# A graph-attention layer on one core: TensorE operands swapped in seven of eight blocks, with the start's order changed

## The reference

```python
# x: 4096 x 128 float32, adj: 4096 x 4096 int32, attn: 256 x 1
s_i = emb @ attn[:d]
s_j = emb @ attn[d:]
e = leaky_relu(s_i + s_j.T, negative_slope=0.2)
e = e + where(adj > 0, 0.0, -1e9)
alpha = softmax(e, axis=1)
out = layernorm(x + alpha @ emb, axis=-1)     # eps 1e-5, emb = x
```

## Time and profile before

| | us |
|---|---|
| median of 3 runs | 259.89 (259.09 to 260.67) |
| the profiled execution's own time | 261.14 |
| its span in the trace | 259.4 |
| PE busy | 249.2 (96%) |
| PEld busy | 241.6 (93%) |
| VectorE busy | 234.4 (90%) |
| ScalarE busy | 169.0 (65%) |
| POOL busy | 36.2 (14%) |
| HBM read and written | 69.21 MB and 2.10 MB, 275 GB/s over the span |

### The profile page before, as it was taken

How to read it: one execution, slowest core, us unless ns; L and a number is a source line. 1 busy time by engine, 2 the same in 40 slices (tenths; PEclk the granted TensorE clock), 3 DMA queues, 4 the chain that set the end, 5 groups by cost and what they waited for, 6 DMA issues and landing times.

```text
span 259.4 us, 5385 instructions
## 1 busy us (share of the span) xinstructions
PE 249.2 (96%) x2117; PEld 241.6 (93%) x2117; DVE 234.4 (90%) x383; ACT 169.0 (65%) x250; POOL 36.2 (14%) x74
## 2 busy tenths in 40 slices
PE   7899999999999999999999999999999999999980
PEld 6556999999999999999999999999999999999970
DVE  1858999999999999999999999999999999999252
ACT  0579999976975797559954795559752986154010
POOL 1000000000330033003300330015000330033022
PEclk9999999999999999999999999999999999999997
DMA  6999999999999999999999999999999991001001
GB/s 202 316 347 348 349 348 347 350 349 346 349 349 357 351 349 359 352 350 320 326 359 345 329 272 364 339 337 295 361 315 326 264 252 42 3 0 44 0 0 44
DMA packets 70237, 71.68 MB, mean 276 GB/s; under 512 B 2881, under 2 KB 68674, under 8 KB 70210
## 3 DMA queue, kind: packets, MB, share of 16 engines
q1 hardware_dynamic: 34594, 34.67, 44.3%
q10 hardware_dynamic: 34592, 34.67, 43.6%
q0 software_dynamic: 1024, 1.97, 2.3%
HBM read 69.21 MB, written 2.10 MB: 275 GB/s over the span
## 4 chain that ended last, share of the span: by engine, by line
PE 89%; ACT 3%; DMA 2%; DVE 1%; POOL 1%; SPq 1%; ACTq 1%; issue 0%; DVEq 0%
PE psum L808 86%; DMA x_raw<-in_x_dram 2%; PE psum L786 1%; PE psum L775 1%; POOL out_dram L259 1%; ACT adj_in L357 1%; ACT mask_bytes L386 1%; ACTq L251 1%; ACT q_row L369 1%; SPq L233 0%; ACT x_raw L470 0%; DVE weights L674 0%; ACT xj L375 0%; DVE mask_t L583 0%; ACT adj_in L348 0%
## 5 line engine op out<-in xcount | busy, mean ns | idle before, releaser
L808 PEld LDWEIGHTS psum<-xj,weights 128*128 128x128 f32 x2048 | 229.1, 192 | 1.5 <-issue 0.9
L808 PE MATMUL psum<-xj,weights 128*128 128x129 f32 x2048 | 229.8, 275 | 0.2 <-DVE weights L674 0.2
L674 DVE SCALAR_TENSOR_TENSOR weights<-q_row,r_j,mask_t 128x512 f32<-128x512 f32 x256 | 172.6, 740 | 1.6
L392 ACT ACTIVATE mask_bytes<-adj_in 128x4096 uint8<-128x4096 int32 x27 | 97.5, 3611 | 28.6 <-DMA adj_in<-in_adj_dram 28.6
L570 DVE STREAM_TRANSPOSE mask_t<-mask_bytes 128x1024 uint32<-128x1024 uint32 x27 | 33.4, 1236 | 0.0
L312 POOL TENSOR_SCALAR neg_mean<-total 128x4 f32<-128x4 f32 x7 | 3.2, 460 | 169.4 <-ACT x_raw L398 169.4
L398 ACT ACTIVATE x_raw<-x_raw 128x128 f32<-128x128 f32 x28 | 8.3, 297 | 22.5 <-DVE x_raw L619 22.5
L321 POOL DMA_DIRECT2D out_dram<-x_raw x28 | 14.6, 527 | 20.5 <-ACT x_raw L412 20.4
L386 ACT ACTIVATE mask_bytes<-adj_in 128x2048 uint8<-128x2048 int32 x9 | 17.1, 1909 | 0.0
L405 ACT ACTIVATE unused<-x_raw,neg_mean 128x128 f32<-128x128 f32 x28 | 10.9, 391 | 4.1 <-POOL neg_mean L312 4.1
L412 ACT ACTIVATE x_raw<-x_raw,offset,rstd 128x128 f32<-128x128 f32 x28 | 11.5, 480 | 2.3 <-POOL offset L318 2.3
(11 more groups left out here) (58 smaller groups left out, 59.8 us busy)
## 6 DMA issues: line engine op xcount, KB each, us to landing
adj_in<-in_adj_dram ACTq DMA_DIRECT2D x64, 512.0 KB, 13.4
adj_in<-in_adj_dram SPq DMA_DIRECT2D x64, 512.0 KB, 13.6
out_dram<-x_raw POOLq DMA_DIRECT2D x28, 64.0 KB, 5.4
x_raw<-in_x_dram ACTq DMA_DIRECT2D x4, 128.0 KB, 3.1
x_raw<-in_x_dram SPq DMA_DIRECT2D x4, 128.0 KB, 3.6
x_raw<-in_x_dram ACTq DMA_DIRECT2D x2, 256.0 KB, 5.8
x_raw<-in_x_dram SPq DMA_DIRECT2D x2, 256.0 KB, 7.1
out_dram<-x_raw POOLq DMA_DIRECT2D x4, 32.0 KB, 1.9
```

The lines of the kernel that those rows point to most:

```text
L392: nc.scalar.activation(mask_bytes[:, g % BYTE_SLOTS, :, :, :], adj_in[:, g % ADJ_SLOTS, :, :, :], ACT.Sign).then_inc(bytes_ready, 1)
L674: nc.vector.scalar_tensor_tensor(weights[:, slot_of(n, c), :], q_row[:, n * BANK:(n + 1) * BANK], r_j[:, c:c + 1], mask_t[:, (n * PIECES + ...
L808: return nc.tensor.matmul(banks[(n * K + t) % 8][:, 0:D1], weights[:, slot_of(n, c), t * P:(t + 1) * P], xj[:, c, 0:D1], start=(c == 0), s ...
```

## The change

It does four things.

1. In blocks 0 to 6 the operands on TensorE are swapped: `xj` of the chunk (128 columns) is stationary and the chunk's 512 weights are the moving operand, one product for a chunk (`block_product`) in place of four. The sums of a block come out with features on partitions and rows along the free axis, in one bank. After a block, ScalarE copies them to SBUF (`take_sums`, 128 x 512), and TensorE turns them back by four transposes (`turn_back`), right after chunk 6 of the next block; `residual` reads those, at chunk 19 in place of 13.
2. 128 columns must now hold the denominator too. `xj` drops the last feature: columns 0 to 126 are `(x - x_127) * d_j`, column 127 is `d_j`. A shift of all features of a row is taken out by the LayerNorm, so feature 127 of `y` is left as `x_127`. `scale_xj` therefore becomes Identity with a bias and a scale operand for each partition; the bias `-x_127 * d_j` is made on POOL. The last block keeps four products for a chunk, now of 128 columns, not 129.
3. At the start, the load of `attn` is issued on SP behind the two transfers of the first `x` part, not before them.
4. Of piece 0's first half, ScalarE converts two of four tiles and VectorE the two others. ScalarE's `q_piece(1)` to `(7)` move behind pieces 3, 4, 5 and 6 (before: 1 to 3 at once, the rest behind pieces 2 and 4). The LayerNorm steps of a block move to fixed distances behind its `take_sums`.

```diff
-    D1 = D + 1
-    PITCH = D + 2
+    DEN = D - 1
...
+    BY_DVE_TILES = 2
...
-    RESIDUAL_AT = 13
+    TURN_BACK_AT = 6
+    RESIDUAL_AT = 19
+    TAKE_SUMS_AT = [4, 9, 13, 18, 22, 27, 31]
+    SUM_ROWS_IN = 3
+    NORMALISE_IN = 4
...
+    SUM_BANK = [3, 2]
+    BACK_BANK = [1, 0]
...
         def _(sp):
 
+            load_x(sp, LOW_HALF, 0)
             sp.dma_start(attn_row_in[:], attn[:, :].rearrange("d o -> o d")).then_inc(attn_loaded, 16)
-            for part in range(X_PARTS):
+            for part in range(1, X_PARTS):
                 load_x(sp, LOW_HALF, part)
...
+            pool.wait_ge(products_ready, STRIPES)
+            nc.gpsimd.tensor_scalar(neg_last[:], x_raw[:, :, DEN], -1.0, 0.0, ALU.mult, ALU.add).then_inc(neg_last_ready, 1)
+            pool.wait_ge(neg_last_ready, 1)
+            pool.wait_ge(factors_ready, 1)
+            nc.gpsimd.tensor_tensor(last_x[:], neg_last[:], d_j[:], ALU.mult).then_inc(last_x_ready, 1)
+            nc.gpsimd.tensor_copy(xj[:, :, DEN], d_j[:]).then_inc(xj_last_ready, 1)
...
-            nc.scalar.activation(xj[:, :, D], below_max[:], ACT.Exp, scale=SLOPE)
...
-                    nc.scalar.activation(xj[:, c, 0:D], x_raw[:, c, :], ACT.Copy, scale=d_j[:, c:c + 1]).then_inc(xj_scaled, 1)
+                    nc.scalar.activation(xj[:, c, 0:DEN], x_raw[:, c, 0:DEN], ACT.Identity, bias=last_x[:, c:c + 1],
+                                         scale=d_j[:, c:c + 1]).then_inc(xj_scaled, 1)
...
+            def take_sums(n):
+
+                act.wait_ge(weights_used, (n + 1) * CHUNKS)
+                if n > 0:
+                    act.wait_ge(turned_back, n)
+                nc.scalar.copy(sums[:], banks[SUM_BANK[n % 2]][:, :]).then_inc(sums_ready, 1)
...
+            act.wait_ge(adj_loaded[0], 16 * Q)
+            nc.scalar.activation(mask_bytes[:, 0, BY_DVE_TILES:K, :, 0:P], adj_in[:, 0, BY_DVE_TILES:K, :, 0:P],
+                                 ACT.Sign).then_inc(quarter_by_act_ready, 1)
             q_piece(0)
-            act.wait_ge(factors_ready, 1)
+            act.wait_ge(last_x_ready, 1)
             scale_xj(0, 1)
-            q_piece(1)
-            q_piece(2)
-            q_piece(3)
...
-                if g == PIECES - 2:
-                    q_piece(4)
-                    q_piece(5)
-                elif g == PIECES:
-                    q_piece(6)
-                    q_piece(7)
-                if g % PIECES == PIECES - 1 and g > PIECES:
-                    sum_rows(g // PIECES - 1)
-                    sum_squares(g // PIECES - 1)
-                if g % PIECES == 0 and g > PIECES:
-                    normalise(g // PIECES - 2)
+                if g == PIECES - 1:
+                    q_piece(1)
+                elif g >= PIECES and 2 * (g - PIECES) + 2 < RB:
+                    q_piece(2 * (g - PIECES) + 2)
+                    q_piece(2 * (g - PIECES) + 3)
+                if g - SUM_ROWS_IN in TAKE_SUMS_AT:
+                    sum_rows(TAKE_SUMS_AT.index(g - SUM_ROWS_IN))
+                    sum_squares(TAKE_SUMS_AT.index(g - SUM_ROWS_IN))
+                if g - NORMALISE_IN in TAKE_SUMS_AT:
+                    normalise(TAKE_SUMS_AT.index(g - NORMALISE_IN))
+                if g in TAKE_SUMS_AT:
+                    take_sums(TAKE_SUMS_AT.index(g))
...
+            def turn_back(n):
+
+                pe.wait_ge(sums_ready, n + 1)
...
+                for t in range(K):
+                    last = nc.tensor.transpose(banks[BACK_BANK[n % 2]][:, t * P:(t + 1) * P], sums[:, t * P:(t + 1) * P], ident[:])
+                last.then_inc(turned_back, 1)
+
+            def block_product(n, c):
+                nc.tensor.matmul(banks[SUM_BANK[n % 2]][:, :], xj[:, c, :], weights[:, slot_of(n, c), :],
+                                 start=(c == 0), stop=(c == CHUNKS - 1)).then_inc(weights_used, 1)
+
+            def product(c, t):
+                return nc.tensor.matmul(banks[((BLOCKS - 1) * K + t) % 8][:, 0:D], weights[:, slot_of(BLOCKS - 1, c), t * P:(t + 1) * P],
+                                        xj[:, c, :], start=(c == 0), stop=(c == CHUNKS - 1))
...
+                    if n > 0 and c == TURN_BACK_AT:
+                        turn_back(n - 1)
```

More of the change, by code:

```diff
@@ L598, in group_of, with sums_of @@
                 return FINAL_GROUPS if n == BLOCKS - 1 else [slice(0, K)]
+            def sums_of(n, t):
+                if n == BLOCKS - 1:
+                    return banks[(n * K + t) % 8][:, 0:P]
+                return banks[BACK_BANK[n % 2]][:, t * P:(t + 1) * P]
             def denominators(n, g):
                 v = group_of(n)[g]
[L602 to L608 removed]
+                if n < BLOCKS - 1:
+                    dve.wait_ge(turned_back, n + 1)
+                    den = banks[BACK_BANK[n % 2]].rearrange("p (t d) -> p t d", d=P)[:, :, DEN]
+                else:
+                    if v.stop < K:
+                        dve.wait_ge(tile_summed, v.stop)
+                    else:
+                        dve.wait_ge(weights_used, (n + 1) * CHUNKS)
+                    bank = (n * K + v.start) % 8
+                    den = psum[:, bank:bank + v.stop - v.start, DEN]
+                nc.vector.tensor_scalar(rden[:, v], den, LEAST, None, ALU.max).then_inc(den_ready, 1)
             def invert(n, g):
@@ L805, in _ @@
                 s_i_piece(rb)
-            def product(n, c, t):
-                return nc.tensor.matmul(banks[(n * K + t) % 8][:, 0:D1], weights[:, slot_of(n, c), t * P:(t + 1) * P],
-                                        xj[:, c, 0:D1], start=(c == 0), stop=(c == CHUNKS - 1))
+            def turn_back(n):
+                pe.wait_ge(sums_ready, n + 1)
+                if n < 2:
+                    pe.wait_ge(q_ready, S_I_BANK.index(BACK_BANK[n]) + 1)
+                else:
+                    pe.wait_ge(y_ready, (n - 1) * K)
+                for t in range(K):
[7 more added lines that the diff above has]
+                                        xj[:, c, :], start=(c == 0), stop=(c == CHUNKS - 1))
             for n in range(BLOCKS):
@@ L816, in _ @@
                         pe.wait_ge(xj_scaled, c + 1)
+                        if c == 0:
+                            pe.wait_ge(xj_last_ready, 1)
                     pe.wait_ge(weights_ready, n * CHUNKS + c + 1)
                     if c == 0:
-                        if n == 1:
-                            pe.wait_ge(q_ready, RB)
-                        elif n > 1:
-                            pe.wait_ge(y_ready, (n - 1) * K)
-                    for t in reversed(range(K)) if n == 0 and c == 0 else range(K):
-                        if n == 0 and c == 0:
-                            pe.wait_ge(q_ready, K - t)
-                        last = product(n, c, t)
-                    last.then_inc(weights_used, 1)
+                        if n < 2:
+                            pe.wait_ge(q_ready, S_I_BANK.index(SUM_BANK[n]) + 1)
+                        elif n < BLOCKS - 1:
+                            pe.wait_ge(sums_ready, n - 1)
+                        else:
+                            pe.wait_ge(q_ready, RB)
+                    if n < BLOCKS - 1:
+                        block_product(n, c)
+                    else:
+                        for t in range(K):
+                            last = product(c, t)
+                        last.then_inc(weights_used, 1)
+                    if n > 0 and c == TURN_BACK_AT:
+                        turn_back(n - 1)
             for t in range(K):
@@ L831, in _ @@
                         pe.wait_ge(weights_ready, (BLOCKS - 1) * CHUNKS + c + 1)
-                    last = product(BLOCKS - 1, c, t)
+                    last = product(c, t)
                     if t == K - 1:
```

30 lines of the change are left out of this document (19 added, 11 removed).

## The result

| | before | changed |
|---|---|---|
| median, us | 259.82 (259.09 to 260.67, 6 runs) | 256.76 (256.41 to 257.97, 6 runs) |
| ratio, with 95% interval | | 0.9898 (0.9866 to 0.9930) |
| the profiled execution: time, span | 261.14, 259.4 | 256.62, 254.8 |
| PE busy | 249.2 | 240.8 |
| PEld busy | 241.6 | 125.9 |

A forecast was written before the change was run, and what follows sets the result against it. TensorE's own stream was taken as the bound, with VectorE only following. From the median of 259.89 us, -7.9 - 0.6 + 3.1 - 0.1 + 0.1 + 2.7 = -2.7 us gave 257.2, range 255.0 to 260.0.

The forecast's parts named there:

- What bounds the kernel: From 25.94 us on TensorE's own stream bounds the kernel, 0.895 us for a chunk; VectorE only follows.
- Wide products: 224 chunks go from 8 records of 129 columns to 2 of 512, 0.895 to 0.860 us each: -7.9 us.
- The last block: Its 256 records of 128 columns step by 0.110 us in place of 0.1119: -0.6 us.
- Turning back: 28 transposes in TensorE's own stream at 0.110 us each: +3.1 us, upper bound 7.6.
- The start: `attn` issued later stays hidden, and SP's first x part goes 0.35 us sooner: -0.1 us.
- The first weights: ScalarE's quarter of piece 0 is complete at 20.13, so TensorE starts at 21.8: +0.1 us.
- ScalarE through block 0: Slower `xj` and `take_sums(0)` make TensorE wait at chunks 14, 30, 38, 54: 3.4 us lost where 0.7 was, +2.7.
- ScalarE keeping up: Rival: the bias operand costs nothing, the loss at chunk 14 shrinks to 0.6 us, 255.6 us in all; chance 0.10.
- Block 1 did not go worse: Rival denied here: pieces 5 to 8 come another 1.5 us late and TensorE stands for that, 258.7 us; chance 0.17.
- The clock did not fall: Rival denied here: two waits in blocks 0 and 1 each drop the clock to 1.2 GHz, 262.6 us; chance 0.05.
- Wide products did gain: Rival denied here: wide products gain nothing, the sum is +5.2 us, 265.1 us; chance 0.04.

The follow-up runs named there:

- the kernel of all three: Changed kernel, but VectorE converts all of piece 0's first half, block 0's sums are copied behind piece 5's bytes, POOL makes 12 `xj` chunks: 254.69 us, ratio 0.9833.

## Why the prediction was right

**The total** was 257.2, in the range of 255.0 to 260.0, and 256.76 was measured: a gain of 3.1 us by the medians, and 2.7 by the ratio, for 2.7. By its own steps:

- *What bounds the kernel*: right. The chain's one long piece of TensorE was the right thing to price; 2.7 us off TensorE's stretch are the gain.
- *Wide products*, -7.9: right (its own factors give -7.84). 0.858 for a chunk against 0.860 forecast and 0.894 before, in a stream with changing stationary matrices.
- *The last block*, -0.6: wrong, it is nothing (its own factors give -0.5). The step failed where it took the transposes' 0.110 for products of 128 columns. They step by 0.1116, as those of 129 did, and the kernel with fewer columns shows that 112, 96 and 64 columns do too.
- *Turning back*, +3.1: right, 0.44 for each of seven. A record's 0.27 us is not what the stream pays: twice as many cost 2.9 us. The Trainium skill's 275 ns (TensorE: Matmul & The Clock Gate, PE-mode transpose), given for bf16, agrees with the record's duration here (273), and an estimate by it of the doubling would be 7.7.
- *The start*, -0.1: too small to tell from nothing; the kernel with `attn` alone measured 1.0008 (0.9996 to 1.0020).
- *The first weights*, +0.1, and the split quarter: within the noise; undoing the quarter changed nothing.
- *ScalarE through block 0*, +2.7: right in place and cause, a little too large. Lost at chunks 14, 30, 38, 54: forecast 1.7, 0.2, 1.1, 0.2; measured 1.30, 0.11, 1.12, 0.09 and restarts. In all 3.2 where 1.0 was lost before, so +2.15. The first entry is smaller by 0.4. The losses came out 0.55 us lower than forecast and the last block gave 0.6 less, so that the two misses of the sum cancel: -7.9 + 0 + 3.1 + 2.15 = -2.65, and 2.7 were measured on the stretch. That the total fits to 0.1 us is luck to that extent.

The prediction gave no reason for the gain, though: it took a chunk's 0.035 us from two rows, and for the last block it took the streamed columns to count. What the runs show is that a narrow record costs 0.1117 us whatever it streams between 64 and 129 columns. Eight of them are 0.894 a chunk, and two wide ones 0.858. The swap wins by the smaller number of records, each with its load, and not by columns. The dropped feature in itself gains nothing (it makes the unswapped kernel 0.55% slower); its use is that 127 features and the denominator fit one stationary matrix.

**The rivals.** ScalarE keeping up did not come; without the bias operand 0.8 (by the stretch) to 1.1 us (by the ratios) more would have been won, 1.6 were forecast. Block 1 did not go worse: nothing was lost after chunk 54. The clock did not fall at the waits of 1.3 and 1.1 us: in the changed kernel's profile it stood at 1.00 from 4.60 us until after the last product. Wide products did gain.

What stays open: whether the load or something else of each record sets the 0.1117 us; how much of the 0.4 us between the medians' gain (3.1) and the stretch's (2.7) is real, since the interval of the ratio is wider than it, and the stretch itself differs by 0.3 between two profiles of nearly the same code; and what decides when the granted clock rises in the start (between 4.45 and 13.86 us in these profiles; in two of them it fell again for 3.4 us).

## What to carry to other kernels

Take the step from start to start of the very instruction and operands that you price, not of one of the same size: here a transpose and a product of 128 columns differ by 2.4 ns, and 256 of them were a term of the sum. Ask whether the streamed columns pace the stream at all, by changing their number in one kernel. If they do not, fewer columns are worth nothing, and fewer records, each with its load, are what can gain. And when an engine near full gets slower instructions, follow its written order piece by piece against the consumer's new pace: the two waits were foreseen to 0.4 us so, and moving one copy and 12 instructions took back another 1.8 us by the ratios.

## What the runs showed of the hardware that was not expected

- A float32 product's records step by 0.1117 us at 64, 96, 112, 128 and 129 streamed columns, and by 0.429 at 512; a transpose of 128 by 0.109.
- In the block of 32 columns a record, the granted clock fell to 0.50 in the fourth chunk, though TensorE had no idle time there and stayed busy for 20.00 of 20 us, and rose again in the next block, of 128 columns. At 0.50 a record steps by 0.213 us.
- On POOL, an `xj` of 128 x 127 elements with two operands for each partition takes between 0.45 and 1.49 us, against 0.48 on ScalarE. In the profile of the kernel of all three the four that take 0.45 to 0.46 start before VectorE's first weight or in VectorE's transposes; the others, 0.89 to 1.49, run beside VectorE's weights. Those weights are slower beside POOL as well: 12 of them take 0.778 us in the mean there, one of them 0.948, against 0.747 in the same stretch of the changed kernel. First POOL's group, then VectorE's weights from 17.66 to 28.74 us with all three and in the changed kernel (ns min/median/max):

```profile
L338 POOL TENSOR_SCALAR xj<-x_raw,d_j,last_x x12: 452/934/1485, 17.7 to 27.8; 128x127 f32<-128x127 f32 x12
L727 DVE SCALAR_TENSOR_TENSOR weights<-q_row,r_j,mask_t x12: 746/756/948, 18.5 to 27.6; 128x512 f32<-128x512 f32 x12
L722 DVE SCALAR_TENSOR_TENSOR weights<-q_row,r_j,mask_t x12: 744/746/752, 18.8 to 27.9; 128x512 f32<-128x512 f32 x12
```
